# Nine gather buffers, a first weight in two loads, an earlier context load, and a last value product in two halves

## What is computed

```python
x = x + attention(layernorm(x), context)        # context: 4 x 1601 x 512, 257 image rows, 1344 text rows
#   q, k_text, k_img: linear + bias, rms norm over 512, times a weight;  v_text, v_img: linear + bias
#   out = softmax(q k_img') v_img + softmax(q k_text') v_text  (16 heads of 32), then linear o
x = x + ffn(layernorm(x))                       # 2048 rows
#   router: sigmoid scores of 32 experts + bias, best 3 of 8 groups, best 4 experts, weights * 2.5
#   each expert takes its first 80 rows: y = (silu(X Wg) * (X Wu)) Wd, times the row's weight, added to the row
#   shared expert of width 512 on every row
```

## Time and profile before

| | us |
|---|---|
| three timed executions | 1218.33, 1219.57, 1220.24 |
| profiled execution, its own time | 1222.39 |
| its span in the profile | 1220.6 |
| PE busy | 1152.7 (94%) |
| DVE busy | 822.1 (67%) |
| ACT busy | 652.0 (53%) |
| POOL busy | 189.6 (16%) |

### The profile page before, as it was taken

One profiled execution on the slowest core, in us unless ns is written; L12 is line 12 of the kernel. 1 busy time (PEld: TensorE's weight loads), 2 busy tenths in 40 slices (PEclk: granted clock), 3 DMA queues, 4 the chain that ended last, 5 costly groups with the idle time before them and its releaser, 6 DMA issues. The chain is left out here.

```text
span 1220.6 us, 20797 instructions
## 1 busy us (share of the span) xinstructions
PE 1152.7 (94%) x8484; PEld 416.4 (34%) x8484; DVE 822.1 (67%) x1038; ACT 652.0 (53%) x920; POOL 189.6 (16%) x299
## 2 busy tenths in 40 slices
PE   6899999999999999999999999997999999999896
PEld 2342222444222244422224442222544433333332
DVE  6775878877677887767798777996778842222121
ACT  5558997444898644498864458894221121221121
POOL 1220000143000013300002320001110011333442
PEclk9999999999999999999999999999999999999998
DMA  9851000449100056800014682013823337999742
GB/s 313 174 104 44 2 2 10 130 116 212 36 2 2 11 129 142 208 15 2 2 48 96 161 186 98 2 36 107 339 70 121 104 104 305 338 320 294 205 71 27
DMA packets 140344, 143.02 MB, mean 117 GB/s; under 512 B 107984, under 2 KB 108240, under 8 KB 135248
## 3 DMA queue, kind: packets, MB, share of 16 engines
q1 hardware_dynamic: 135120, 130.78, 36.7%
q0 software_dynamic: 5120, 10.82, 4.6%
HBM read 95.67 MB, written 20.73 MB: 95 GB/s over the span
## 5 line engine op out<-in xcount | busy, mean ns | idle before, releaser
L658 ACT ACTIVATE work<-ps 128x1024 f32<-128x1024 f32 (+1 forms) x416 | 403.0, 1021 | 41.3 <-PE ps L1126 37.4
L1132 PE MATMUL ps<-work,vals 128*32 128x512 f32 (+2 forms) x1664 | 221.0, 603 | 0.9 <-ACT work L658 0.6
L981 PE MATMUL ps<-wts,work 128*128 128x512 f16 x864 | 193.2, 379 | 2.8 <-DVE work L716 2.5
L1126 PE MATMUL ps<-quer,keys 32*128 32x512 f16 x2496 | 171.9, 377 | 17.7 <-ACT work L658 4.5
L891 DVE TENSOR_TENSOR work<-work 128x2048 f32<-128x2048 f32 x64 | 146.6, 2291 | 6.7 <-DVE work L891 0.5
L891 DVE TENSOR_TENSOR attn<-attn,work 128x2048 f32<-128x2048 f32 x62 | 142.0, 2290 | 5.2
L981 PE MATMUL ps<-wts,hl 128*128 128x512 f16 x480 | 112.4, 385 | 12.7 <-DVE wts L698 6.9
L981 PEld LDWEIGHTS ps<-wts,work 128*128 128x128 f16 x864 | 84.0, 98 | 110.1 <-issue 9.0
L1935 PE MATMUL ps<-wring,xgt 128*80 128x512 f32 x256 | 114.9, 592 | 0.0
L1761 DVE COPY xgt<-ps 128x320 f32<-128x320 f32 x32 | 15.7, 492 | 145.2 <-PE ps L1926 145.2
L579 ACT CAST work<-work 128x512 f16<-128x512 f32 x68 | 42.0, 618 | 129.3 <-DVE work L748 129.3
(11 more groups left out here) (213 smaller groups left out, 1348.3 us busy)
## 6 DMA issues: line engine op xcount, KB each, us to landing
wring<-in_wx SPq DMA_DIRECT2D x32, 1536.0 KB, 9.1
raw<-in_ctx SPq DMA_DIRECT2D x52, 256.0 KB, 3.1
work<-in_x SPq DMA_DIRECT2D x4, 1024.0 KB, 5.4
table<-nums SPq DMA_DIRECT2D x16, 256.0 KB, 2.4
work<-in_x SPq DMA_DIRECT2D x12, 256.0 KB, 5.2
x<-work SPq DMA_DIRECT2D x12, 256.0 KB, 2.6
x2t_rows<-nums SPq DMA_DIRECT2D x12, 256.0 KB, 2.5
x2t<-x2t_rows SPq DMA_DIRECT2D x3, 1024.0 KB, 9.0
```

The source lines that it names most:

```text
L658: act.activation(prob[0:rows, s % PROBS, 2 * half:2 * half + 2, :], ps[0:rows, 2 * pair:2 * pair + 2, :], ACT.Exp, scale=SCALE).then_inc(a ...
L981: mm = pe.matmul(out, lhs(a, c)[:, cols], wts[:, w, z, c * D:(c + 1) * D], start=(k == 0), stop=(k == len(steps) - 1))
L1126: mm = pe.matmul(ps[:, 2 * pair + h % 2, :], k[h * HD:(h + 1) * HD, :], q[h * HD:(h + 1) * HD, :], start=(e == 0), stop=(e == len(terms) - 1))
L1132: return pe.matmul(ps[h * HD:(h + 1) * HD, NUM, :], vals[a:z, ORDER[n], g * P + h * HD:g * P + (h + 1) * HD], prob[a:z, s % PROBS, h, :], ...
```

## The change

It has four parts. (1) Nine gather buffers in place of six; three are put where the router's scratch was. (2) WKI is loaded in two parts of 1024 columns, 4 KB a row; ACT still converts it in four pieces. (3) In batch 0 the load of context tile 4 is put right behind that of tile 3, ahead of x, WQ and two bias rows, so SP waits there for `ctx_low` of tile 2; ACT and DVE convert tile 3 in slot 1 and not in slot 2, DVE ahead of the low half of WV. (4) The last value product is done in two halves of 6 matmuls, one between `scores(0)` and `scores(1)`, one behind `scores(1)`; DVE, not ACT, copies it out, at the end of its projection list. Some semaphores are merged, with no change of order.

```diff
-GATHERS = 6
+GATHERS = 9
...
                 load_ctx(p * B, 0, 0)
-                for part in range(NC):
-                    load_part(WKI, part, NC, (s_w[WKI], s_fw[0], s_fw[1], s_fw[2])[part])
+                for part in range(2):
+                    load_part(WKI, part, 2, (s_w[WKI], s_fw[0])[part])
                 load_ctx(p * B, 0, 1)
...
-                        if k is not None and k + 2 < KT and k > 0:
+                        if k is not None and k + 2 < KT and k > 0 and (b > 0 or k != 2):
                             sp.wait_ge(c_lo, kvn(bb, k))
                             load_ctx(bb, b, k + 2)
+                        if b == 0 and k == 1:
+                            sp.wait_ge(c_lo, kvn(bb, 2))
+                            load_ctx(bb, b, 4)
                         if b == 0 and i == 1:
                             load_x(bb, b)
                             load_weight(WQ)
...
                 for i in range(SLOTS):
-                    if i + 1 in KV_AT and (b > 0 or i > 1):
+                    if i + 1 in KV_AT and (b > 0 or i > 2):
                         ctx_high(bb, KV_AT[i + 1])
...
-                    if b == 0 and i == 0:
-                        ctx_high(bb, 2)
+                    if b == 0 and i <= 1:
+                        ctx_high(bb, 2 + i)
                     key_square(bb, i)
...
-                    if bb < B and s == 0:
-                        value_out(bb, KT - 1)
...
                     if i > 0 or b == 0:
                         key_raw(bb, i)
+                    if b == 0 and i == 1:
+                        ctx_low(bb, 3)
                     if b == 0 and i <= 1:
                         weight_low(p, (WK, WV)[i])
...
                 key_norm(bb, SLOTS - 1)
                 key_low(bb, SLOTS - 1)
+                if bb < B:
+                    value_out(bb, KT - 1)
...
                 scores(0)
                 if p == 0:
-                    value(bb, KT - 1)
+                    last_value(bb, 0)
                 scores(1)
+                if p == 0:
+                    last_value(bb, 1)
```

More of the change, by code:

```diff
@@ L149, in __init__ @@
                       for i, o in enumerate((132, 144, 156, 168, 84, 96, 64, 48, 24, 182, 0, 12))]
-        self.xg = [at(f"xg{i}", 112 * KB_ + 2176 * i, [CAP, TROW], F32) for i in range(GATHERS)]
+        self.xg = [at(f"xg{i}", 112 * KB_ + 2176 * i if i < 6 else 40 * KB_ + 2176 * (i - 6), [CAP, TROW], F32)
+                   for i in range(GATHERS)]
         self.xgt = [at(f"xgt{i}", 124 * KB_ + 768 + 1280 * i, [P, NC, CAP], F32) for i in range(2)]
@@ L544, in first_weight_high @@
             def first_weight_high(p):
-                for part, sem in enumerate((s_w[WKI], s_fw[0], s_fw[1], s_fw[2])):
-                    act.wait_ge(sem, 16 * (p + 1 if part == 0 else 2 * p + 1))
+                for part in range(NC):
+                    if part == 0:
+                        act.wait_ge(s_w[WKI], 16 * (p + 1))
+                    if part == 2:
+                        act.wait_ge(s_fw[0], 16 * (2 * p + 1))
                     cols = slice(part * D, (part + 1) * D)
@@ L814, in project @@
                 for i in range(SLOTS):
-                    if i + 1 in KV_AT and i > (0 if b > 0 else 1):
+                    if i + 1 in KV_AT and i > (0 if b > 0 else 2):
                         ctx_low(bb, KV_AT[i + 1])
@@ L902, in sums_and_results, with value_out @@
                 dve.reciprocal(rcp[:, :], ps[:, DEN, :]).then_inc(a_rcp, 1)
+            def value_out(bb, k):
+                dve.wait_ge(v_mm, kvn(bb, k))
+                dve.tensor_scalar(vals[:, ORDER[k], :], ps[:, value_bank(k), :], 1.0 / WS, None, ALU.mult).then_inc(v_out, 1)
             def check_sums(b):
@@ L1021, in key, with last_value @@
                             None).then_inc(k_mm, 1)
+            def last_value(bb, half):
+                if half == 0:
+                    pe.wait_ge(v_out, kvn(bb, KT - 3))
+                    if bb % B > 0:
+                        pe.wait_ge(o_out, xn(out_batch(bb - 1), 2))
+                lhs = ctx_lhs(KT - 1)
+                for c in (2 * half, 2 * half + 1):
+                    for a, z in PARTS:
+                        mm = pe.matmul(ps[:, NUM, :], lhs(a, c), wts[:, WV, z, c * D:(c + 1) * D],
+                                       start=(c == 0 and (a, z) == PARTS[0]), stop=(c == NC - 1 and (a, z) == PARTS[-1]))
+                if half == 1:
+                    mm.then_inc(v_mm, 1)
             def value(bb, k):
@@ L1316, in ffn_program @@
         e_r, e_ez, link = event("e_r"), event("e_ez"), event("link")
-        e_m16, e_pos, e_oh, e_ar, e_wv, e_idx = (event(n) for n in (
-            "e_m16", "e_pos", "e_oh", "e_ar", "e_wv", "e_idx"))
+        e_mask, e_oh, e_ar, e_idx = (event(n) for n in ("e_mask", "e_oh", "e_ar", "e_idx"))
         e_a2 = event("e_a2")
@@ L1630, in _ @@
             out_low(2)
-            dve.wait_ge(s_r, 32)
+            dve.wait_ge(s_xl, 32)
             chain(dve.tensor_scalar(rwt[:, 0, :], rraw[:, :], WS, None, ALU.mult))
@@ L1703, in _ @@
             counted(6, NT)
-            dve.sem_inc(e_m16, 1)
+            dve.sem_inc(e_mask, 1)
             gate(8)
@@ L1724, in _ @@
             chain(TT(fl(wv), fl(wv), fl(tmp), ALU.mult))
-            dve.sem_inc(e_wv, 1)
+            dve.sem_inc(e_mask, 1)
             for n in (9, 10):
@@ L1747, in _ @@
             gate_low(13)
-            dve.wait_ge(s_xl, 16 * B)
+            dve.wait_ge(s_xl, 32 + 16 * B)
             chain(dve.tensor_scalar(ib[:, :], ia[:, :], 0.0, None, ALU.is_equal))
@@ L1894, in _ @@
             pe.wait_ge(s_const, N_CONST)
-            pe.wait_ge(e_m16, 1)
+            pe.wait_ge(e_mask, 1)
             flat = lambda t: t[:, :, :].rearrange("p j e -> p (j e)")
@@ L1898, in _ @@
             pe.matmul(ps[:, POSITION, :], before[:, :], flat(m16), start=True, stop=False)
-            pe.matmul(ps[:, POSITION, :], ones16[:, :], flat(c16), start=False, stop=True).then_inc(e_pos, 1)
+            pe.matmul(ps[:, POSITION, :], ones16[:, :], flat(c16), start=False, stop=True).then_inc(e_r, 1)
             down_next(1, 2)
```

13 lines of the change are left out of this document (6 added, 7 removed).

## The result

| | kernel before | changed kernel |
|---|---|---|
| median, 20 runs each in turns | 1219.2 us | 1214.12 us |
| lowest to highest | 1214.2 to 1225.3 | 1211.7 to 1217.3 |
| profiled execution, own time | 1222.39 | 1214.52 |
| its span | 1220.6 | 1212.8 |

The ratio is 0.9956, with a 95% interval from 0.9947 to 0.9966: 0.44% faster, some 5 us. In two later series of six runs each the changed kernel's medians were 1212.8 and 1212.13 us; over all 32 runs it is 1213.3. The prediction said 1208.2, with 1204.5 to 1213.0 as its range. So the sign was right, and the gain was a little under half of the forecast 11.4 us.

A forecast was written before the change was run, and what follows sets the result against it. PE, busy 94%, was held by late gathers, start-up loads and ACT/PE alternation. Gains 7.6 + 4.0 + 1.0 = 12.6 us off 1222.39 gave 1209.8, less 2.8 for the median 1207.0, adjusted for stalls to 1208.2; range 1204.5 to 1213.0.

The forecast's parts named there:

- the slack formula: Expert loop: nine buffers leave gathers 27.2 us minus the scatter backlog, 9.5 us at worst, so none is late.
- the added issues: Ahead of scatter 0: three more gather issues, 0.92 us each, fit in POOL's 21.55 us idle; uncovered they cost 3.7.
- the 7.6 us: Expert loop: PE's lateness from gather stalls, 6.4 us waiting and the rest mostly lower clock, all removed by nine buffers.
- a middle: Stall term for ordinary runs: worth 4.8 to 7.6 us, so the forecast was set at 1208.2 rather than 1207.0.
- rival A: Expert loop: ACT's waits for landed scatters before reusing four result buffers delay PE; 1212.4 us, chance 0.15.
- the ring of four: Expert loop: ACT writes result n only after scatter n-4 lands; result 21 would be 1.6 us late, unfelt by PE.
- each 0.1 of pace costs 1.8 us: Expert loop: price of slower scatters over 18 experts, counted from a pace of 6.96 us on.
- my rate of packets: First weight's load at the start: packet rate limits traffic, so 4 KB rows reach up to 410 GB/s; gain 1.6 us.
- rival C: Batch 0: context tile 4's lead is given back at tile 5 or later, 1.5 of 4.0 us stay; 1210.7, chance 0.15.
- D: Expert loop: scatters fall far behind and the kernel gets slower, 1226.9 us at a pace of 8.0; chance 0.03.
- E: Expert loop: gathers are late in the DMA queue, not POOL's list, and stay late; 1214.6 us, chance 0.04.
- B: First weight's load at the start: loading it in two parts brings nothing; 1209.8 us, chance 0.2.

The follow-up runs named there:

- e10: Changed kernel with eight gather buffers instead of nine; median 1213.0 us, ratio 0.9936 to the kernel before.
- e11: Changed kernel with seven gather buffers instead of nine; median 1212.86 us, ratio 0.9943 to the kernel before.
- e12: Kernel before, loading only half of each expert's weights from expert 12 on (for its time alone); median 1215.07 us, ratio 0.9955.
- e1: Kernel before with only the nine gather buffers added; median 1215.04 us, ratio 0.9964.
- e5: Changed kernel, unchanged, measured again; median 1212.8 us, ratio 0.9938 to the kernel before.
- e7: Changed kernel with the three added gathers issued later, just ahead of the first scatter; median 1213.65 us, ratio 0.9942 to the kernel before.
- e8: Changed kernel with the first weight in four loads again; median 1212.84 us, ratio 0.9934 to the kernel before.
- e17: Changed kernel, unchanged, run in turns with e18; median 1212.13 us, ratio 0.9948 to the kernel before.
- e14: Changed kernel with halved expert weight loads, first weight in four loads again; median 1212.10 us, 0.8 above the same kernel with all parts.
- e16: Changed kernel with halved expert weight loads, last value product in one piece, copied on ACT; median 1212.37 us, 1.1 above the same kernel with all parts.
- e9: Changed kernel with six result buffers instead of four; median 1210.79 us, ratio 0.9919 to the kernel before.
- e18: Changed kernel with six result buffers instead of four, run in turns with e17; median 1211.27 us, ratio 0.9938 to the kernel before.

## Why the prediction was wrong

**What bounds the kernel, and part 1's mechanism: right.** The waits for gathers and the lower clock behind them are gone, the turns are 5.90 us apart, the slack formula put eight buffers on the safe side and seven past the edge, as e10 and e11 have it, and the added issues cost nothing under POOL's idle time (24.61 us at the head in every profile but one).

**The first step that failed is how the 7.6 us of the profiled execution were carried over to an ordinary run.** I took 7.6 off 1222.39, and then 2.8 more because that execution was above the median, and gave 1.2 back as "a middle". But the execution was above the median because of its stalls. e12 shows it: without stalls the kernel before takes 1215.07, and 1222.39 - 7.6 is 1214.8. So nothing of the 2.8 lay elsewhere, and the term was 5.0 and not 6.4; my lower bound, 4.8, was the honest value. The four later profiles with six buffers had 5.0, 9.4, 0 and 7.9 us of excess. One profile can't show that its largest stall varies by chance, but its distance from the median was the hint, and I had it.

**The second is the chance of rival A.** I treated the pace of 6.89 us as a property of the kernel. Over 15 profiles with full loads it ran from 6.62 to 7.29, and in five it was above the 6.96 at which I let the ring of four take over. Seven of the 15 had four result buffers and eight or nine gather buffers; there PE lost 0, 0.5, 0, 6.7, 1.4, 0.8 and 0.3 us in the loop (the first profile, e1, e5, e7, e8, e10, e17), 1.4 in the mean. Its price was sized well: for e7's 7.29 the rule of "each 0.1 of pace costs 1.8 us" gives 5.9, measured 6.7; only the onset is softer, as e1, e10 and e17 lost 0.5, 0.8 and 0.3 us at 6.90, 6.92 and 6.95. So it is not one case with one price: it takes some executions more and some less, and its part of the median is 0.9 to 2.5 us.

**The third is part 2: 1.6 forecast, 0.8 to 0.9 measured.** The traffic with two loads rose as I said, but not to 410 GB/s. One profile of each, 3 to 5 and 5 to 7 us, the two that lie furthest apart at 5 to 7; the last columns are the granted clock, the share of the DMA engines' time and GB/s. With four loads (e14):

```profile
3.00:5.00 2.00, 0.00 (x0) 0.00 (x0) 1.85 (x17) 0.64 (x2) 0.00 (x0) 1.00 0.92 291
5.00:7.00 2.00, 0.57 (x2) 0.28 (x3) 1.46 (x3) 1.23 (x2) 0.00 (x0) 1.00 0.62 161
```

With two (e17):

```profile
3.00:5.00 2.00, 0.00 (x0) 0.00 (x0) 1.85 (x17) 0.62 (x1) 0.00 (x0) 1.00 0.97 292
5.00:7.00 2.00, 0.00 (x0) 0.01 (x1) 0.92 (x3) 1.15 (x2) 0.00 (x0) 1.00 1.02 397
```

In the mean of seven profiles each, the traffic went from 254 and 212 GB/s to 286 and 353, and at 9 to 11 us it fell from 399 to 338. All in all 0.2 MB more had moved by 11 us, some 0.5 us of traffic. The engines' share in 3 to 7 us was 0.81 with four loads and 0.95 with two: idle time of the DMA engines shrank, which my rate of packets didn't tell from slow packets. The Trainium skill's rule in "DMA: Bandwidth & Descriptors", section "Why small descriptors are slow (HBM only)", gave under 0.1 us. For the packets themselves it fits better than my rate: by the trace's packet records a row of 2 KB took 84 ns in the median and one of 4 KB 159, so two short ones cost 6% more than a long one, 0.14 us over the 512 rows of this weight on 16 engines. But it leaves out the engines' idle time, and by it part 2 comes out 0.7 us too small. The first pair of profiles, 17.12 against 17.08 us, seemed to prove it right; that pair was chance.

What left the DMA engines idle isn't shown, and I overlooked one candidate. SP's issues of WKI and then of WVI, before and in the changed kernel:

```profile
1.25 1.84 SPq L323 DMA_DIRECT2D nums<-in_w  x4
...
3.60 0.93 SPq L323 DMA_DIRECT2D nums<-in_w  x2
```

```profile
1.24 0.89 SPq L324 DMA_DIRECT2D nums<-in_w  x2
...
2.65 1.12 SPq L324 DMA_DIRECT2D nums<-in_w  x2
```

Two issues less put everything up to WVI 0.95 us earlier in the queue, in all 13 profiles with two loads against the seven with four, and that is about the size of the gain. No run separates it from what the rows' length does; two loads with SP held back by 0.95 us would.

**Part 3: right.** 2.2 us against 2.4. One thing moved that the sum didn't have. POOL's step in tile 1's norm, a single column, takes 0.19 us in the median of its 68 times, but 2.26 here, and DVE's norm waited 0.45 us for it. In all 14 profiles with part 3 it took 2.26 or 2.27 us, in the six without 1.40 or 1.41, and in all 20 it ended 0.04 to 0.06 us behind DVE's low half of WV:

```profile
24.17 2.28 DVE L716 SCALAR_TENSOR_TENSOR wts<-attn,wts 128x2048 f16<-128x2048 f32 x1
24.24 2.26 POOL L494 TENSOR_SCALAR small<-small 128x1 f32<-128x1 f32 x1 [6.97 <-ACT work L591]
```

Part 3 puts that operation of DVE right ahead of POOL's step. That POOL is held until it ends is what the 20 pairs of times suggest; no run tests it. The load was early enough, and the lead stayed to the end of the batch: rival C didn't come.

**Part 4: right.** 0.8 us by the profiles and 1.1 by e16, against 1.0. The numerators start 5.28 us behind the product; forecast were 5.2, and it was 5.40. The copy is what they wait for, as forecast. Timeline, batch 1 of the changed kernel, against the earlier trace rows:

```profile
303.20 1.47 PE L1044 MATMUL ps<-wts,hl 128*128 128x512 f16 x6
...
305.42 0.83 PE L1152 MATMUL ps<-quer,keys 32*128 32x512 f16 x12 [0.75 <-ACT work L665]
306.18 1.47 PE L1044 MATMUL ps<-wts,hl 128*128 128x512 f16 x6
307.58 0.83 PE L1152 MATMUL ps<-quer,keys 32*128 32x512 f16 x12
307.68 0.69 DVE L915 TENSOR_SCALAR vals<-ps 128x512 f32<-128x512 f32 x1 [2.52 <-PE ps L1044]
...
308.48 1.06 PE L1158 MATMUL ps<-work,vals 128*32 128x512 f32 x8
```

**The sum again**, off the shown median: 1219.57 - 5.0 - 0.8 - 2.2 - 0.8 = 1210.8, which is where e9 and e18 are, 1210.79 and 1211.27. With 0.9 to 2.5 us for the ring of four it is 1211.7 to 1213.3; e5 and e17 are at 1212.8 and 1212.13. The first series was at 1214.12, 5.9 us above the forecast. The term for the stalls, 6.4 against 5.0, makes 1.4 of that, the ring of four 0.9 to 2.5, part 2 0.8, parts 3 and 4 0.2 each; 0.8 to 2.4 us stay unexplained.

**The range** left out D and E rightly: no profile had a pace of 7.6, and with nine buffers no gather was late. Its upper end was too low: it took A, B and C one at a time, and it had no term for the variation of the pace. Its lower end is a little under its own sum, as 7.6 + 4.3 + 2.0 us off 1219.57 is 1205.7 and not 1205.

## What to carry to other kernels

Before the stalls of one profiled execution are taken off a median, ask how often they occur: where the execution lies above the median, the excess and the stall are likely the same microseconds and may be subtracted once. Where two rings hang on one slow transfer, deepening the first hands the lateness to the second; size both for the slowest pace seen, since the added buffers cost no time here and the pace varies. A part worth a microsecond is measured in a variant of the kernel from which the noise was removed, or as the mean of one step over many profiles, not from one pair. Such a mean says that a step came earlier, but not why: look also at what the issuing engine does earlier.

## What the runs showed of the hardware

- The pace of scatters that add to memory, each waiting for the last one to land, was 6.62 to 7.29 us beside 1.5 MB of weight loads an expert, and 5.90, PE's own, beside half of that. It varied between executions of the same program (6.83, 6.84 and 6.95 for the changed kernel). Once the weight loads were over it was 4.12 to 4.23 in all 15 profiles.
- Delaying three gathers by some 13 us, ahead of the first scatter (e7), came with the slowest pace of all, 7.29. One profile: whether it is more than chance is open.
- One execution in 20 had DVE held up at the head of the loop, by 1.85 us in all, with nothing in the trace that accounts for it.
- A first weight in four loads of 2 KB rows left the DMA engines idle for 19% of 3 to 7 us, one in two loads of 4 KB rows for 5% (means of seven profiles each). SP took 1.84 us to issue the four and 0.89 for the two.
- A one-column step of POOL that takes 0.19 us in the median took 1.40 to 2.27 beside a 2.28 us operation of DVE on 128x2048, and ended 0.04 to 0.06 us behind it in all 20 profiles.
